# Attention with heads of 64: the order of units on three engines

## The reference

```python
def _L2_xattn_ref(x, context, Wq, Wk, Wv, Wo, bo):      # 8 heads of 64
    q, k, v = heads(x @ Wq), heads(context @ Wk), heads(context @ Wv)
    attn = softmax(einsum('bhnd,bhmd->bhnm', q, k) * 64 ** -0.5)
    return merge(einsum('bhnm,bhmd->bhnd', attn, v)) @ Wo + bo

def _L3_attn_ref(inputs, W_qkv, W_out):                 # 32 query heads on 16 key/value heads of 64
    q, k, v = split_heads(inputs @ W_qkv); k, v = repeat(k, 2), repeat(v, 2)
    scores = einsum('bhqd,bhkd->bhqk', q, k) / sqrt(64) + slopes * (k_pos - q_pos)
    attn = softmax(where(causal, scores, -inf))
    return merge(einsum('bhqk,bhkd->bhqd', attn, v)) @ W_out

x = x + block(_layernorm(x))
```

## Time and profile before

| what | value |
|---|---|
| median of 3 runs | 11427.36 us (11424.93 to 11432.99) |
| the profiled execution | 11425.49 us, span 11423.7 us |
| c2: stretch in the span | 7430 to 7926 us, 16 groups |
| a3: stretch in the span | 8750 to 10226 us, 16 groups |
| busy over the span | PE 72%, DVE 68%, ACT 35%, POOL 21% |

### The profile page before, as it was taken

The page is one execution under the profiler, slowest core; times in us unless marked ns, Lnnn a source line. Parts: engine busy times, 40 slices in busy tenths (PEclk is TensorE's granted clock), DMA queues, the critical chain, the costliest instruction groups (busy, mean ns, idle before and its releaser), DMA issues. The chain is left out here.

```text
span 11423.7 us, 161141 instructions
## 1 busy us (share of the span) xinstructions
PE 8266.7 (72%) x60044; PEld 5107.7 (45%) x60044; DVE 7803.2 (68%) x11217; ACT 3955.6 (35%) x5327; POOL 2452.7 (21%) x821
## 2 busy tenths in 40 slices
PE   5666888476767656777777777787668777776689
PEld 4544555343445422322223333455445555554466
DVE  6655544587878844888878888456775766766644
ACT  3333333211111044444444444433333333333333
POOL 0000000153536601555555555000000000000000
PEclk7777866576677777888888888898669999987799
DMA  0000000000000000111111111000000000000000
GB/s 18 0 9 6 5 1 0 14 0 0 0 0 0 0 8 17 53 53 51 53 47 52 55 54 52 8 8 7 0 2 19 2 2 2 2 6 7 6 8 15
DMA packets 83848, 184.37 MB, mean 16 GB/s; under 512 B 16186, under 2 KB 38564, under 8 KB 82628
## 3 DMA queue, kind: packets, MB, share of 16 engines
q1 hardware_dynamic: 83524, 180.01, 4.8%
HBM read 172.57 MB, written 7.41 MB: 16 GB/s over the span
## 5 line engine op out<-in xcount | busy, mean ns | idle before, releaser
L1847 POOL TENSOR_TENSOR m_dBx<-m_dtx,m_Bs 128x1024 f32<-128x1024 f32 x516 | 1247.0, 2419 | 870.8 <-DVE m_hs L2140 847.8
L2140 DVE TENSOR_TENSOR_SCAN m_hs<-m_ps_dA,m_dBx 128x512 f32<-128x512 f32 x1032 | 1202.8, 1207 | 173.3 <-POOL m_dBx L1847 123.0
L1952 PE MATMUL m_ps_y<-m_yc,ident 128*128 128x512 f32 x2064 | 1202.4, 714 | 0.0
L2023 ACT ACTIVATE m_ps_dA<-m_dt,m_A 128x504 f32<-128x504 f32 x1032 | 688.9, 679 | 1395.8 <-DVE m_hs L2140 1385.1
L2481 PE MATMUL x_ps_p<-Y,ident 128*128 128x256 f32 (+1 forms) x1920 | 713.6, 546 | 379.8 <-DVE Y L2398 215.0
L2481 PEld LDWEIGHTS x_ps_p<-Y,ident 128*128 128x128 f32 x1920 | 425.5, 243 | 660.4 <-issue 246.6
L2146 DVE TENSOR_TENSOR m_yc<-m_hs,m_ps_C 128x1024 f32<-128x1024 f32 x516 | 630.2, 1221 | 107.7 <-issue 90.9
L1935 PE MATMUL m_ps_C<-m_parts,m_sel 128*128 128x512 bf16 x518 | 230.3, 445 | 630.0 <-DVE m_yc L2146 629.1
L1952 PEld LDWEIGHTS m_ps_y<-m_yc,ident 128*128 128x128 f32 x2064 | 468.9, 229 | 381.5 <-issue 357.2
L547 POOL MEMSET c_vbd<- 128x1152 f32 x2 | 2.1, 1063 | 2928.3 <-POOLq L56 2928.3
L2404 POOL TENSOR_TENSOR Y<-x_score,x_v 128x1024 f32<-128x1024 f32 (+1 forms) x72 | 476.0, 6646 | 237.0 <-DVE x_most L2784 159.7
(11 more groups left out here) (693 smaller groups left out, 18708.2 us busy)
## 6 DMA issues: line engine op xcount, KB each, us to landing
m_Bs<-m_B_rows SPq DMA_DIRECT2D x258, 512.0 KB, 3.5
c_kvb<-in_ctxT SPq DMA_DIRECT2D x50, 256.0 KB, 2.5
out_dram<-X SPq DMA_DIRECT2D x1, 4096.0 KB
m_B_rows<-m_low SPq DMA_DIRECT2D x34, 32.0 KB, 3.2
c_table<-in_table SPq DMA_DIRECT2D x2, 512.0 KB
focus_rows<-X SPq DMA_DIRECT2D x2, 512.0 KB, 9.6
x_xb<-in_ctx SPq DMA_DIRECT2D x1, 1024.0 KB, 15.0
x_xa<-focus_rows SPq DMA_DIRECT2D x1, 1024.0 KB, 6.1
```

The source lines that it names most:

```text
L1847: return nc.gpsimd.tensor_tensor(to, one, other, ALU.mult)
L1952: last = nc.tensor.matmul(ps_y[:, m, :], C.ident[:], yc[:, s % 2, m, :], start=s == 0, stop=s == NS - 1)
L2023: nc.scalar.activation(seqs(ps_dA[:, h % 3, :]), seqs(dt[:, par, m, :]), ACT.Exp, scale=A[:, m, s:s + 1]).then_inc(decay, 1)
L2140: nc.vector.tensor_tensor_scan(h[:, m, :], ps_dA[:, (2 * s + m) % 3, :], dBx[:, s % 2, m, :], 0.0, ALU.mult, ALU.add).then_inc(scanned, 1)
```

## The change

The same instructions are issued; their order changes on three engines.

- VectorE: all value chunks are taken right after `shift(0)`; in c2 the next front comes directly after them, in a3 it comes after `normalise(5)` instead of `shift(7)`. At each x `shift(x+1)` comes before `normalise(x)`, with a wait in front for `pT_done` of unit x-1 (the transposes that read the same half of `s1`). At the last x there is a drain instead.
- TensorE: the scores of units 0 and 1 are made before the loop over units, those of x+2 at x. The front's transposes of the next group come at x=UPI-2; the first two projections of the next group come behind `project_output(i, UPI-2)` of the last x instead of ahead of `turn_probs`.
- ScalarE: Exp(0) comes before the last takes, then Exp(x+1) at x. The front's copy is at x=UPI-2.

```diff
--- before.py
+++ after.py
@@ -1435,11 +1435,20 @@
                 queries_keys(i, 0)
                 for c in range(NQK, NQK + 4):
                     project(i, c)
+                queries_keys(i, 1)
+                for c in range(NQK + 4, NC_):
+                    project(i, c)
+                for taken in (act_taken, dve_taken):
+                    pe.wait_ge(taken, i * (NC_ // 2) + NC_ // 2)
                 for x in range(UPI):
-                    if x + 1 < UPI:
-                        queries_keys(i, x + 1)
-                    else:
+                    if x + 2 < UPI:
+                        queries_keys(i, x + 2)
+                    elif x + 1 < UPI:
                         fr.pe(pe, i + 1)
+                    turn_probs(i, x)
+                    if x > 0:
+                        project_output(i, x - 1)
+                    if x + 1 == UPI:
                         pe.wait_ge(fr.xT_ready, i + 2)
                         if cross:
                             pe.wait_ge(shifted, i * UPI + UPI)
@@ -1447,14 +1456,6 @@
                             pe.wait_ge(scores_read, i * UPI + UPI + 1)
                         project(i + 1, 0)
                         project(i + 1, 1)
-                    if x == 0:
-                        for c in range(NQK + 4, NC_):
-                            project(i, c)
-                        for taken in (act_taken, dve_taken):
-                            pe.wait_ge(taken, i * (NC_ // 2) + NC_ // 2)
-                    turn_probs(i, x)
-                    if x > 0:
-                        project_output(i, x - 1)
                     weigh_values(i, x)
                 project(i + 1, 2)
                 project(i + 1, 3)
@@ -1483,17 +1484,21 @@
                 act.wait_ge(oT_done, i * UPI + x + 1)
                 nc.scalar.activation(oT[:].rearrange("p t j q -> p t (j q)"), ps_o[:], ACT.Copy).then_inc(oT_ready, 1)
 
+            def exponential(i, x):
+                act.wait_ge(shifted, i * UPI + x + 1)
+                nc.scalar.activation(s1[:, x % 2, :, :, :], s1[:, x % 2, :, :, :], ACT.Exp).then_inc(exped, 1)
+
             fr.act(act, 0)
             with act.Fori(0, C.NG) as i:
                 take(act, act_copy, act_scaled, i, 0, 0, NQK + 4)
+                exponential(i, 0)
+                take(act, act_copy, act_scaled, i, 0, NQK + 4, NC_)
                 for x in range(UPI):
-                    act.wait_ge(shifted, i * UPI + x + 1)
-                    nc.scalar.activation(s1[:, x % 2, :, :, :], s1[:, x % 2, :, :, :], ACT.Exp).then_inc(exped, 1)
-                    if x == 0:
-                        take(act, act_copy, act_scaled, i, 0, NQK + 4, NC_)
+                    if x + 1 < UPI:
+                        exponential(i, x + 1)
                     if x > 0:
                         output_copy(i, x - 1)
-                    if x == UPI - 1:
+                    if x == UPI - 2:
                         fr.act(act, i + 1)
                     act.wait_ge(pT_done, i * UPI + x + 1)
                     nc.scalar.activation(pT[:].rearrange("p t j q -> p t (j q)"), ps_t[:], ACT.Copy).then_inc(pT_ready, 1)
@@ -1554,13 +1559,18 @@
                 take(dve, dve_copy, dve_scaled, i, 1, EARLY, NQK)
                 shift(i, 0)
                 take(dve, dve_copy, dve_scaled, i, 1, NQK, NQK + 4)
+                take(dve, dve_copy, dve_scaled, i, 1, NQK + 4, NC_)
+                if UPI == 2:
+                    fr.dve(i + 1)
                 for x in range(UPI):
+                    if x + 1 < UPI:
+                        if x > 0:
+                            dve.wait_ge(pT_done, i * UPI + x)
+                        shift(i, x + 1)
+                    else:
+                        dve.drain()
                     normalise(i, x)
-                    if x == 0:
-                        take(dve, dve_copy, dve_scaled, i, 1, NQK + 4, NC_)
-                    if x + 1 < UPI:
-                        shift(i, x + 1)
-                    if x == UPI - 2:
+                    if x == UPI - 3:
                         fr.dve(i + 1)
                     if x % HG == 0 and x > 0:
                         residual(i, x // HG - 1)
```

## The result

The changed kernel took 11669.09 us (median of 4 runs, 11664.17 to 11676.38), against 11426.15 before (4 runs, 11420.73 to 11432.99). The ratio is 1.0213, with a 95% interval from 1.0195 to 1.0231: 243 us slower. The forecast was 11652, with a range from 11570 to 11760.

The account below looks back on a forecast made before the run. VectorE's loop was taken to bound the middle of a3, TensorE's chain the end of a c2 group; +152 us in a3 and +73 in c2 made +225 on 11427.4, so 11652, range 11570 to 11760.

Parts of the forecast that it names:

- (a): In a3, VectorE's stand for ScalarE's Exp ahead of normalise would go: a gain of 6.7 us a group.
- (b): In a3, VectorE would wait for transposes ahead of shift, 2.15 + 4.3 + 0.35 us a group, and 3.8 at the residual.
- (c): In a3, VectorE's last two takes of V chunks, now before the units, would idle it 2.6 us a group.
- (d): At an a3 group's end, unit 6's transposes and values and unit 5's outputs precede TensorE's last steps: +2.9 us.
- (e): In c2, normalise(0) behind shift(1) delays TensorE's transposes of unit 0, with low clock added: +4.6 us a group.
- Cheap waits, or a boundary cost covered: Rival: cheap waits, high clock throughout, or V takes or tail covered: +100 to +160 us, 11530 to 11590; chance 0.12.
- TensorE the bound: Rival: longer gaps, more low clock, TensorE becomes the bound with a unit near 8 us: 11790; chance 0.10.
- Faster: Rival: transposes hide, their wait before shift under Exp's 1.20 us, so VectorE just loses its Exp stands: 11320; chance 0.04.
- No change: Rival: TensorE, the busier engine, is the bound and its work is the same: 11427; chance 0.04.

Follow-up runs that it names:

- the kernel with the filler: The changed kernel plus unread TensorE matmuls ahead of the transposes of unit 0, four in c2 and two in a3: ratio 1.0182 to the kernel before.
- the three parts of s1: The changed kernel with s1 in three parts instead of two in a3, shift(x+1) waiting for unit x-2: ratio 1.0083 to the kernel before.

## Why the prediction was right, point by point

The forecast had 225 us and the medians differ by 243. That it is only 18 off is in part luck: the groups grew by 255 us, 30 more than forecast, and c2 happened to begin 11 us earlier. Both stages were sized about 0.9 us a group too small (a3 9.5 against 10.4, c2 4.6 against 5.5), and by the points below the low clock of TensorE is most of what was missed.

**(a) Exp hidden, 6.7 us a group: right.** The wait is gone from a3.

**(b) The transposes on VectorE's path: the mechanism right, the size too small.** The middle of an a3 group, which answers to the earlier trace rows: a stand at the high clock, then the residual's wait, then the stand ahead of `shift(7)`:

```profile
9495.05 1.10 PE L1385 MATMUL a_ps_t<-ident,a_s 128*128 128x128 f32 x8 [1.51 <-DVE a_s L1549]
...
9496.27 1.29 DVE L1524 TENSOR_TENSOR a_s<-a_ps_s,a_table 128x512 f32<-128x512 f32 x2 [1.28 <-PE a_ps_t L1385]
...
9501.70 1.23 DVE L1549 TENSOR_TENSOR a_s<-a_s,a_den 128x1024 f32<-128x1024 f32 x1
...
9502.98 1.09 PE L1385 MATMUL a_ps_t<-ident,a_s 128*128 128x128 f32 x8 [3.09 <-DVE a_s L1549]
...
9503.91 1.95 PE L1415 MATMUL a_ps_out<-a_wo,a_oT 128*128 128x128 f32 x16
...
9506.02 0.42 DVE L1554 TENSOR_TENSOR X<-a_ps_out,X 128x256 f32 x1 [3.10 <-PE a_ps_out L1415]
...
9513.06 1.97 PE L1385 MATMUL a_ps_t<-ident,a_s 128*128 128x128 f32 x8 [4.11 <-DVE a_s L1549]
...
9515.15 1.29 DVE L1524 TENSOR_TENSOR a_s<-a_ps_s,a_table 128x512 f32<-128x512 f32 x2 [1.12 <-PE a_ps_t L1385]
```

`normalise(4)` ends at 9502.93, the transposes start at 9502.98 and take 1.09 us; then the output matmuls take 1.95, and only after them comes the residual (L1554), 3.1 us after `normalise`, and behind it `shift(6)` at 9506.36. The residual's waits are 80.5 us in all, of which the second one of a group takes 1.22 as before; 61 us are left, 3.8 a group, 3.9 with the overlap, where the forecast had 3.8. That is a mean: 3.1 where the matmuls ran at the high clock (10 of 16 groups), 4.6 to 5.6 in the others.

The waits of the additions are 126.0 us, with the overlap of 0.08 five times a group 8.3 us a group. The forecast had 2.15 + 4.3 + 0.35 = 6.8. By place in the group (means over 16 groups, with the overlap) they are 2.23 ahead of `shift(2)`, 4.85 ahead of the next three, and 1.19 ahead of `shift(7)`. More than half of what is missing is the last, forecast at 0.35 and at most 1.05: the residual's wait leaves TensorE idle for 4.1 us, and the transposes of unit 5 behind it took 1.97 in 14 groups and 1.84 and 1.96 in the other two, so that the front covers only half of them. The rest is the way back from the transposes to VectorE, which was taken as 0.05 us and is 0.12 in these rows (the transposes end at 9496.15, the additions start at 9496.27), and the mean of the transposes, taken from before at 1.24 us:

```profile
L1385 PE MATMUL a_ps_t<-ident,a_s 128*128 128x128 f32 x1024 | 182.7, 336 | 306.3 <-DVE a_s L1549 306.3
```

182.7 us for 128 units are 1.43. The share of units that meet the low clock is itself moved by the change, and the forecast held it fixed; its sentence that busy times stay the same was wrong for TensorE, by 118 us.

The stand ahead of `shift(2)` was taken at the low clock, 2.15. The beginning of a group (takes of V L1474, additions L1524, last step of `normalise` L1549), which answers to the earlier trace rows:

```profile
9460.49 0.69 DVE L1474 COPY a_val<-a_ps_t 128x512 f32<-128x512 f32 x1 [1.44 <-PE a_ps_t L1358]
...
9462.21 0.69 DVE L1474 COPY a_val<-a_ps_o 128x512 f32<-128x512 f32 x1 [1.02 <-PE a_ps_o L1358]
9462.81 1.28 DVE L1524 TENSOR_TENSOR a_s<-a_ps_s,a_table 128x512 f32<-128x512 f32 x2
...
9468.23 1.23 DVE L1549 TENSOR_TENSOR a_s<-a_s,a_den 128x1024 f32<-128x1024 f32 x1
...
9469.51 1.97 PE L1385 MATMUL a_ps_t<-ident,a_s 128*128 128x128 f32 x8 [3.30 <-DVE a_s L1549]
...
9471.61 1.29 DVE L1524 TENSOR_TENSOR a_s<-a_ps_s,a_table 128x512 f32<-128x512 f32 x2 [2.15 <-PE a_ps_t L1385]
```

Transposes of 1.97 behind a gap of 3.30, and a stand of 2.15. The gap was to be 4.3; it was 3.3 here, because the scores ahead of it ran at the low clock as well, and up to 4.1 in other groups; the transposes took 1.97 in all 16. The forecast had read this from one row with a gap of 2.9, and that was partly luck: in a3 before, only 6 of 42 such rows with a gap of 2.9 to 3.1 took 1.97 throughout, and 23 stayed at the high clock. The sentence cited from the Trainium skill (TensorE: Matmul & The Clock Gate, "Why this matters for your kernels") is borne out for these long gaps by the kernel with the filler, where the same transposes ran at the high clock in 11 of 16 groups.

**(c) The takes of V: right.** In the same rows VectorE takes at 9460.49 and 9462.21 with nothing between, behind waits of 1.44 and 1.02; over a3 they are 23.0 + 16.4 = 39.4 us, 2.5 a group, 2.6 with the overlap of the two, as forecast.

**(d) The end of the group: right.** This answers to the earlier trace rows:

```profile
9521.87 1.09 PE L1385 MATMUL a_ps_t<-ident,a_s 128*128 128x128 f32 x8 [1.56 <-DVE a_s L1549]
...
9522.80 1.95 PE L1415 MATMUL a_ps_out<-a_wo,a_oT 128*128 128x128 f32 x16
...
9523.52 1.23 DVE L1549 TENSOR_TENSOR a_s<-a_s,a_den 128x1024 f32<-128x1024 f32 x1
...
9525.71 1.09 PE L1385 MATMUL a_ps_t<-ident,a_s 128*128 128x128 f32 x8
...
9528.81 1.88 PE L1353 MATMUL a_ps_s<-a_xnT,a_wq 128*128 128x512 f32 x4
...
9533.48 1.95 PE L1415 MATMUL a_ps_out<-a_wo,a_oT 128*128 128x128 f32 x16
```

`normalise(7)` ends at 9524.75, the last output matmuls at 9535.43: 10.7 us, against 8.0 before. That is 2.7, where 2.9 were forecast. The row is as told: transposes, outputs and values of unit 6 come first, the projections at 9528.81 behind the outputs.

With 8.3 for the transposes, 3.9 for the residual and 2.6 for the takes VectorE stands 14.8 us a group; less 6.7, plus 2.7 (read from one group), makes 10.8, and 10.4 were measured (9.5 forecast).

**(e) c2: the mechanism right, 5.5 us instead of 4.6.** It answers to the earlier trace rows:

```profile
7682.95 1.29 DVE L1537 TENSOR_TENSOR c_s<-c_ps_s,c_mx 128x512 f32<-128x512 f32 x2
7684.15 1.21 DVE L1545 TENSOR_REDUCE c_den<-c_s 128x16 f32<-128x1024 f32 x1
...
7685.77 1.23 DVE L1549 TENSOR_TENSOR c_s<-c_s,c_den 128x1024 f32<-128x1024 f32 x1
...
7687.05 1.97 PE L1385 MATMUL c_ps_t<-ident,c_s 128*128 128x128 f32 x8 [4.66 <-DVE c_s L1549]
...
7690.22 1.99 PE L1402 MATMUL c_ps_o<-c_pT,c_val 64*64 64x64 f32 x64 [1.21 <-ACT c_pT L1504]
...
7692.13 1.97 PE L1385 MATMUL c_ps_t<-ident,c_s 128*128 128x128 f32 x8
...
7693.89 1.91 PE L1415 MATMUL c_ps_out<-c_wo,c_oT 128*128 128x128 f32 x8
...
7699.77 1.16 PE L1402 MATMUL c_ps_o<-c_pT,c_val 64*64 64x64 f32 x64
```

`normalise(0)` (L1545 to L1549) follows `shift(1)` and ends at 7687.00; the transposes start at 7687.05, with a gap of 4.66 ahead of them (4.7 forecast), and run at the low clock, as do the values (1.99). What the forecast had only in its high end is that the low clock lasts: the transposes of unit 1 took 1.97 and the first output matmuls 1.91, where before it was 1.04 (in 15 of 16 groups; the row below) and 1.06:

```profile
7693.67 1.04 PE L1385 MATMUL c_ps_t<-ident,c_s 128*128 128x128 f32 x8
```

From the transposes of unit 0 to the values of unit 1 it is 12.7 us in this group, against 11.66 from 7685.79 to 7697.45. This is one of the longer groups. Over all of them the transposes of unit 0 come 5.3 us later, to the digit of the forecast, and the row behind them takes 12.1 us on the mean (11.3 to 12.7) against 11.9 before (10.7 to 14.5); the forecast had it 0.7 shorter. That term, the low clock behind the gap, is what was sized too small in c2.

**The rivals.** *Cheap waits, or a boundary cost covered*: each boundary cost showed up near its size. *TensorE the bound*: the clock fell from 0.93 to 0.87, so its first half came true, but the three parts of s1 freed 9.1 us a group with next to no waiting for scores, so its second half didn't. (Its "near 8 us" for a unit at the low clock was too low: transposes of 1.97 and outputs of 3.62, with values of 1.99 and scores of 1.96 in the changed kernel, add up to 9.5.) *Faster*: the stand would have had to be below 1.20 us with its overlap; directly behind `normalise` the shortest is 1.27 without it, 1.35 with it. *No change*: the busier engine gained 118 us of busy time and the kernel lost 243; TensorE's instructions were the same, and one wait added on VectorE to the kernel before moved a3's group from 93.4 to 105.8 us.

## What to carry to other kernels

Hiding one wait by running a step ahead needs a buffer for the step ahead: with only two halves, the wait for the helper engine in the middle (1.1 us) was exchanged for the wait for the reader of the old half (1.3 to 2.2 us), which had been free as long as it lay beside other work. So name, for each buffer that the new order overwrites earlier, who reads it last and which instruction releases that reader; if it is the one right ahead, nothing hides it. And count what the order of the middle costs at both ends of the loop: here the ends cost as much as the middle could have won, and the new order in the middle, with a third buffer and the takes and the residual moved, with the old order at the end and in c2, was 0.7% faster than the kernel before and 2.8% faster than the change.

## What the runs showed of the hardware

A delay on another engine can cost TensorE more than its length. A wait of 1.29 us on VectorE in c2 made two projections take 3.78 us instead of 1.98 in all 16 groups, where before only 4 took over 3.5, and the group 3.2 us longer. The opposite held as well: matmuls without use, put into a gap, four of them (3.60 us) in c2 and two in a3, made the groups 2.3 and 1.4 us shorter. A gap doesn't bring the low clock every time: in a3 before, 23 of 42 transpose rows behind gaps of 2.9 to 3.1 us stayed at 1.09. TensorE's durations from a profile hold only for the gaps that the kernel had there; over a3 the mean of the eight transposes was 1.24 us at a granted clock of 0.93, 1.43 at 0.87, and again 1.24 (158.5 us for 128 units) at 0.94.
